# Expert loop of an AdaLN block: numbers kept in registers, parts of the last tile not scattered, the last tile finished in two halves

## The chip, the cores and the metric

One NeuronCore of a Trainium2 chip runs the whole program as one launch. The metric is the device time of a launch in microseconds. The program was run three times for its times, and once more with the hardware profiler on.

## The reference

The block takes 4096 tokens of 256 channels. It applies a modulated layer norm and a linear attention over two key/value sets, adds the gated result to the tokens, applies a second modulated layer norm and then a mixture of experts:

```
scores = sigmoid(xf @ gate_w + bias)
top_scores, top_idx = top_k(scores, 2)          # 8 experts, 2 for each token, weights normalised
up  = xf @ up_w[e] + up_b[e];  hact = gelu(up)   # 256 -> 1024
eo  = hact @ down_w[e] + down_b[e]               # 1024 -> 256
combined = sum over e of 0.1 * w[token, e] * eo[token, e]
shared   = 0.1 * (gelu(xf @ sw_up + sb_up) @ sw_down + sb_down)
out = shared + combined;  out = out / (max(|out|) + 1e-6)      # the maximum over the channels of a token
x   = x + gate * out
```

The maximum makes the last step need a token's whole sum: the shared part and both experts' parts.

## The kernel before, in words

Earlier phases leave in DRAM, for each expert, a region with the rows of its tokens (`expert_in`, 256 channels and 16 numbers of metadata: the token, its eight weights, where its part goes, and at which rows its two copies stand). They leave the shared part of each token in the first half of a row of `shared_part` (`sx`, two times 256 channels) and zeros in the second half; `out` already holds the tokens before the last addition.

The last phase goes over tiles of 256 rows, one expert after the other. An expert's last tile is moved back so that it ends with the expert's rows, and rows that the tile before has already handled are masked. With 8192 rows there are at least FULL = 32 tiles and at most ET = 39; how many there are is known only at run time. Tables made on the chip (`etab` expert, `ktab` its rank, `stab` weight slot or 2 for "not needed", `rtab` row, `ntab` next expert, `vtab`) tell each engine what tile j is. An engine reads one number with `entry`, which is a register load from the table, a register operation on it and a range assertion, all at line 981. `tiles` (L1760) lays out the tiles for each engine: four in line, a loop for tiles 4 to 29, two in line, and then tiles 32 to 38, nested, each inside an `If` on `stab[j]`: `unneeded(j)` (L1785) guards the wind-up `last(j)`, `needed(j)` (L1781) guards `body(j)`. With these inputs tiles 0 to 33 are needed, so the last tile is 33.

The five queues, each in program order, for a tile j with u = j % 2:

- SP loads rows (L985) and metadata (L988).
- TensorE in `body(j)` computes the up products of tile j+1 (`up`, L1870), then four transposes for tile j+2 (`turn_h`, L1842) and the down products of tile j (`down`, L1895), into `psY`.
- ScalarE in `body(j)` first does `part_out(j-1)`: after `yc` it scales by the token's weight into `ys` (L1952). Then come `chunks(j+1)`: gelu (L1933), a rounded copy `gTh` (L1938), and `high` (L1926).
- VectorE in `body(j)` first does `start`: `result(j-1)`, which reads `psY` and adds the bias into `yc` (L2019), and `total(j-1)`, which sums the two halves of the gathered row into `bs` (L2026) and adds the weighted `yc` into `sm` (L2032, once for each 128 rows). Then `end`: low parts `gTl` of the next tile (L1998), between them `largest(j-1)` (`top`, L2037 to L2041) and `gated(j-1)` (`fin`, L2046), then `low(j+2)` (L1993), then `targets(j)`: the row numbers `widx` and `oidx` (L2007 to L2013).
- GpSimd in `body(j)` waits for `ix_ok`, `y_ok` and `g_in`, scatters `ys` of tile j into `shared_part` (L2132, one indirect DMA for each 128 rows), gathers the rows of tile j+1 into `gx` (L2123, likewise two), waits until `fin` of tile j is there and adds it into `out` (L2142, likewise two).

A row goes into `out` only where this tile holds the token's second expert; where it holds the first, its part goes to `shared_part`, so that the tile with the second finds it there. When the first tile of an expert is gathered, `vtab` makes the gather wait for the scatter of the tile before; within an expert it doesn't, since a token is there once. After the last needed tile, VectorE's `last` does `start` and `end`, ScalarE's `last` does `part_out`, and GpSimd's `last` waits until all has landed.

## Time and profile before

| | us |
|---|---|
| median of 3 runs | 898.3 |
| lowest, highest | 893.7, 900.07 |
| the profiled execution | 894.99 |
| its span, first to last instruction | 893.2 |
| mean granted TensorE clock | 0.981 of full |

The span is what the trace covers; all starts in the rows below are microseconds from its beginning. PE is TensorE (PEld its weight loads), DVE VectorE, ACT ScalarE, POOL GpSimd. A `q` behind an engine's name (DVEq) is its sequencer, which runs register, branch and semaphore instructions and is not counted as busy.

### The profile page before, as it was taken

How to read it: one execution, taken by the hardware profiler on the slowest of the kernel's cores; microseconds unless marked ns; L12 is line 12 of the kernel's file. 1: busy time of each engine (PE TensorE's matmuls, PEld its weight loads, DVE VectorE, ACT ScalarE, POOL GpSimd, SP SyncE). 2: the span in 40 equal slices, each digit the busy share in tenths (PEclk: the TensorE clock that was granted, in tenths of full speed). 3: DMA queues.
4: the chain of work that ended last, by engine and by line, in shares of the span. 5: the costliest groups of instructions: out<-in, count | busy, mean ns of one | idle time of the engine just before them, and what ended most of it. 6: DMA issues, size and time to landing. Idle time of an engine off the chain costs nothing.

```text
span 893.2 us, 21239 instructions
## 1 busy us (share of the span) xinstructions
PE 838.0 (94%) x5989; PEld 777.0 (87%) x5990; DVE 632.6 (71%) x1663; ACT 473.9 (53%) x880; POOL 404.9 (45%) x415
## 2 busy tenths in 40 slices
PE   5999999899999999999989999989999999999982
PEld 5778887788888888889789999989999999999982
DVE  5788977568877677687867666666666666666663
ACT  3865654254544544445457665555555556665540
POOL 4553310211451441441701666654666665666665
PEclk9999999899999999999999999999999999999996
DMA  8220000471241231230671333352444433344542
GB/s 294 73 95 1 1 1 0 121 215 25 98 121 26 98 104 39 100 91 32 220 262 53 96 85 97 90 183 55 92 92 95 93 93 89 75 85 91 98 99 51
DMA packets 68607, 83.30 MB, mean 93 GB/s; under 512 B 23088, under 2 KB 56842, under 8 KB 68400
## 3 DMA queue, kind: packets, MB, share of 16 engines
q0 software_dynamic: 25792, 39.92, 19.2%
q1 hardware_dynamic: 41920, 41.64, 15.0%
q8 instruction: 37, 0.61, 0.3%
q10 hardware_dynamic: 816, 0.79, 0.3%
q14 instruction: 42, 0.34, 0.1%
HBM read 45.44 MB, written 41.55 MB: 97 GB/s over the span
## 4 chain that ended last, share of the span: by engine, by line
PE 27%; issue 6%; DVE 5%; DMA 4%; ACT 3%; DVEq 2%; POOL 2%; ACTq 1%; POOLq 0%
PE psUp L1870 14%; PE psY L1895 12%; DMA gx<-shared_part,meta 3%; DVEq L981 1%; ACT gu L1933 1%; DMA shared_part<-ys,widx 1%; PE psH L1842 1%; DVE gTl L1998 1%; POOL out L2142 1%; ACT gTh L1938 1%; DVE top L2037 1%; DVE yc L2019 1%; POOL shared_part L2132 0%; DVE bs L2026 0%; DVE eT L1993 0%
## 5 line engine op out<-in xcount | busy, mean ns | idle before, releaser
L1870 PE MATMUL psUp<-eT,wup 128*128 128x256 f32 x1632 | 203.2, 284 | 6.0 <-DVE eT L1993 5.5
L1870 PEld LDWEIGHTS psUp<-eT,wup 128*128 128x128 f32 x1632 | 198.5, 192 | 7.7 <-issue 6.0
L1895 PE MATMUL psY<-wdn,gTh 128*128 128x256 f32 x1088 | 200.5, 286 | 0.0
L1895 PEld LDWEIGHTS psY<-wdn,gTh 128*128 128x128 f32 x1088 | 169.4, 192 | 0.0
L1895 PE MATMUL psY<-wdn,gTl 128*128 128x256 f32 x544 | 154.3, 284 | 0.0
L2142 POOL DMA_INDIRECT out<-fin,oidx x68 | 109.4, 1609 | 23.5 <-issue 15.5
L1952 ACT ACTIVATE ys<-yc,meta 128x256 f32<-128x256 f32 x68 | 30.9, 502 | 162.6 <-DVE yc L2019 162.6
L1933 ACT ACTIVATE gu<-psUp,ubias 128x256 f32<-128x256 f32 x272 | 113.4, 468 | 6.6 <-DVE gTl L1998 4.1
L1998 DVE TENSOR_TENSOR gTl<-gu,gTh 128x512 fp32r<-128x512 f32 x136 | 93.7, 689 | 26.0 <-ACT gTh L1938 23.6
L2123 POOL DMA_INDIRECT gx<-shared_part,meta x68 | 68.6, 1009 | 84.8 <-DMA shared_part<-ys,widx 63.4
L2132 POOL DMA_INDIRECT shared_part<-ys,widx x68 | 71.4, 1049 | 76.6 <-ACT ys L1952 40.0
L1895 PEld LDWEIGHTS psY<-wdn,gTl 128*128 128x128 f32 x544 | 104.2, 192 | 0.0
L1161 PE MATMUL psU<-h2T,su 128*128 128x512 f32 x384 | 100.3, 399 | 0.0
L1173 PE MATMUL psY<-sd,ghi 128*128 128x256 f32 x512 | 96.8, 288 | 3.0 <-DVE glo L1404 3.0
L1252 ACT ACTIVATE gf<-psU,sbu 128x512 f32<-128x512 f32 x64 | 44.1, 690 | 100.6 <-PE psU L1161 93.3
L1173 PEld LDWEIGHTS psY<-sd,ghi 128*128 128x128 f32 x512 | 81.8, 191 | 8.9 <-DVE glo L1404 5.9
L1674 POOL DMA_INDIRECT expert_in<-h,post x64 | 65.7, 1026 | 52.5 <-DVEq L1476 30.2
L1938 ACT CAST gTh<-gu 128x512 fp32r<-128x512 f32 x136 | 84.4, 621 | 4.3
L1161 PEld LDWEIGHTS psU<-h2T,su 128*128 128x128 f32 x384 | 68.9, 189 | 13.3
L1173 PE MATMUL psY<-sd,glo 128*128 128x256 f32 x256 | 72.8, 284 | 0.0
L2019 DVE TENSOR_TENSOR yc<-psY,dbias 128x512 f32<-128x512 f32 x34 | 23.5, 691 | 67.3 <-issue 63.5
L611 PE MATMUL psG<-xn,kn 128*128 128x257 f32 x256 | 61.5, 389 | 0.8 <-DVE kn L780 0.8
(303 smaller groups left out, 1376.2 us busy)
## 6 DMA issues: line engine op xcount, KB each, us to landing
hin<-expert_in SPq DMA_DIRECT2D x36, 256.0 KB
X<-in_L_attn_x SPq DMA_DIRECT2D x8, 512.0 KB, 7.6
X<-bo_row POOLq DMA_DIRECT2D x8, 512.0 KB
shared_part<-prow SPq DMA_DIRECT2D x8, 512.0 KB, 6.7
shared_part<-sh SPq DMA_DIRECT2D x8, 512.0 KB
out<-X SPq DMA_DIRECT2D x8, 512.0 KB, 4.3
raw_up<-in_L_ffn_up_w SPq DMA_DIRECT2D x3, 1024.0 KB, 6.0
raw_dn<-in_L_ffn_down_w SPq DMA_DIRECT2D x3, 1024.0 KB, 10.4
```

The lines of the kernel that those rows point to most:

```text
L611: mm = nc.tensor.matmul(psG[:, j, 0:C + 1], kn[:, t, j * P:(j + 1) * P], xn[:, f % XR, t], start=(f == 0 and t == 0), stop=(f == NG - 1 an ...
L1161: mm = nc.tensor.matmul(psU[:, m % 2], su[:, b, k, m * P:(m + 1) * P], h2T[:, r, a, k], start=(n == 0), stop=(n == 5))
L1173: mm = nc.tensor.matmul(psY[:, t // 2, (t % 2) * C:(t % 2 + 1) * C], lhs, sd[:, b, m], start=(m == 0 and t % 2 == 0 and n == 0), stop=(m = ...
L1674: nc.gpsimd.indirect_dma_start(out=hs[:, :], out_offset=bass.IndirectOffsetOnAxis(ap=post[:, r, t, k:k + 1], axis=0), in_=h2[:, r, t], in_ ...
L1870: mm = nc.tensor.matmul(psU[:, c, (m % 2) * TR:(m % 2 + 1) * TR], wup[s][:, a, k, m * P:(m + 1) * P], eT[:, u, b, k], start=(n == 0), stop ...
L1895: mm = nc.tensor.matmul(psE[:, u, h * C:(h + 1) * C], (gTh, gTl)[a][:, u, m, h * P:(h + 1) * P], wdn[s][:, b, m], start=(n == 0), stop=(n ...
L1933: nc.scalar.activation(gu[:, c % 2, m], psU[:, c, m * TR:(m + 1) * TR], ACT.Gelu, bias=ubias[:, bass.ds(e * MK + 2 * c + m, 1)]).then_inc( ...
L1938: nc.scalar.copy(gTh[:, u, 2 * c:2 * c + 2], gu[:, c % 2]).then_inc(eu_hi, 1)
L1998: nc.vector.tensor_tensor(gTl[:, u, 2 * c:2 * c + 2], gu[:, c % 2], f32(gTh[:, u, 2 * c:2 * c + 2]), ALU.subtract).then_inc(eu_lo, 1)
L2123: nc.gpsimd.indirect_dma_start(out=gx[:, u, h], out_offset=None, in_=sx[:, :], in_offset=token).then_inc(g_in[u], 16)
L2132: nc.gpsimd.indirect_dma_start(out=sx_half[:, :], out_offset=first, in_=ys[:, u, h], in_offset=None, bounds_check=2 * N - 1, oob_is_err=Fa ...
L2142: nc.gpsimd.indirect_dma_start(out=out[0], out_offset=token, in_=fin[:, u, h], in_offset=None, bounds_check=N - 1, oob_is_err=False, compu ...
```

## The change

A helper `known` reads a table entry for tiles from FULL on once for each engine and keeps the register; later uses take it from there. GpSimd's scatter of parts moves inside the `If` that asks whether the next tile is needed, so the last tile's parts are computed and scattered no more; ScalarE loses its `last`. The semaphore of the gather becomes one for each 128 rows. VectorE's `last` does the last tile in two halves of 128 rows with `finish`, and GpSimd's addition into `out` waits for each half by itself, in every tile. VectorE loads `etab[j]` before `targets(j)` for tiles from 32 on.

```diff
-    g_in = [sem(f"g_in{i}") for i in range(2)]
+    g_in = [[sem(f"g_in{i}{h}") for h in range(2)] for i in range(2)]
...
+    held = {}
+
+    def known(eng, table, j, most):
+
+        if not isinstance(j, int) or j < FULL:
+            return entry(eng, table, j, most)
+        key = (eng.engine, table.name, j)
+        for old in [k for k in held if k[0] == eng.engine and k[2] < j - 2]:
+            del held[old]
+        if key not in held:
+            held[key] = entry(eng, table, j, most)
+        return held[key]
...
     def needed(eng, j):
 
-        return eng.If_ne(eng.to_reg(entry(eng, stab, j, 2)), 2)
+        return eng.If_ne(eng.to_reg(known(eng, stab, j, 2)), 2)
 
     def unneeded(eng, j):
 
-        return eng.If_eq(eng.to_reg(entry(eng, stab, j, 2)), 2)
+        return eng.If_eq(eng.to_reg(known(eng, stab, j, 2)), 2)
...
-                k_exp = entry(pe, ktab, j, E)
+                k_exp = known(pe, ktab, j, E)
                 if isinstance(j, int) and j >= FULL:
-                    return entry(pe, stab, j, 2), k_exp
+                    return known(pe, stab, j, 2), k_exp
...
-            def last(j):
-
-                part_out(j - 1, 1 - j % 2, (j - 1) // 2, entry(act, etab, j - 1, E - 1))
-
             def body(j, u, more, i):
                 new = entry(act, ntab, j, E - 1)
                 if more:
-                    e1 = entry(act, etab, j + 1, E - 1)
+                    e1 = known(act, etab, j + 1, E - 1)
                 if later(j, 1):
-                    part_out(j - 1, 1 - u, i - 1 + u, entry(act, etab, j - 1, E - 1))
+                    part_out(j - 1, 1 - u, i - 1 + u, known(act, etab, j - 1, E - 1))
...
-            tiles(act, body, last)
+            tiles(act, body)
...
             def total(j, u, landed, e):
-                wait(dve, g_in[u], landed)
+                for h in range(2):
+                    wait(dve, g_in[u][h], landed)
...
             def start(j, u, i):
-                e = entry(dve, etab, j - 1, E - 1)
+                e = known(dve, etab, j - 1, E - 1)
                 result(j - 1, 1 - u, e)
-                total(j - 1, 1 - u, 32 * i + 32 * u, e)
+                total(j - 1, 1 - u, 16 * i + 16 * u, e)
+
+            def finish(j, u, landed, h, e):
+
+                done = 3 * j + 3 * h
+                wait(dve, g_in[u][h], landed)
+                if not h:
+                    wait(dve, s_ok, 2 * j)
+                    wait(dve, f_s, 2 * j)
+                nc.vector.tensor_tensor(bs[:, h], gx[:, u, h, C:2 * C], gx[:, u, h, 0:C], ALU.add).then_inc(b_ok, 1)
+                wait(dve, ey_ev, j + 1)
+                wait(dve, b_ok, j + 1 + h)
+                nc.vector.scalar_tensor_tensor(sm[:, h], yc[:, h], meta[:, u, h, bass.ds(e + 1, 1)], bs[:, h],
+                                               ALU.mult, ALU.add).then_inc(s_ok, 1)
+                wait(dve, s_ok, 2 * j + h + 1)
+                nc.vector.tensor_reduce(top[:, 0, h:h + 1], sm[:, h], AX.X, ALU.max, apply_absolute_value=True
+                                        ).then_inc(f_c, 1)
+                wait(dve, f_c, done + 1)
+                nc.vector.tensor_scalar(top[:, 0, h:h + 1], top[:, 0, h:h + 1], EPS, None, ALU.add).then_inc(f_c, 1)
+                wait(dve, f_c, done + 2)
+                nc.vector.reciprocal(top[:, 1, h:h + 1], top[:, 0, h:h + 1]).then_inc(f_c, 1)
+                wait(dve, f_c, done + 3)
+                nc.vector.scalar_tensor_tensor(fin[:, u, h], sm[:, h], top[:, 1, h:h + 1], gate_fb[:],
+                                               ALU.mult, ALU.mult).then_inc(f_s, 1)
 
             def last(j):
 
-                start(j, j % 2, j // 2)
-                end(j, j % 2, False)
+                u, i = j % 2, j // 2
+                e = known(dve, etab, j - 1, E - 1)
+                result(j - 1, 1 - u, e)
+                for h in range(2):
+                    finish(j - 1, 1 - u, 16 * i + 16 * u, h, e)
...
+                if isinstance(j, int) and j >= FULL:
+                    known(dve, etab, j, E - 1)
                 targets(j, u, i)
                 ahead(j, new, (1,))
...
             def body(j, u, more, i):
+                def parts():
+                    wait(pool, y_ok, 2 * j + 2)
+                    for h in range(2):
+                        wait(pool, g_in[u][h], 16 * i + 16)
+                    for h in range(2):
+                        first = bass.IndirectOffsetOnAxis(ap=widx[:, u, h:h + 1], axis=0)
+                        nc.gpsimd.indirect_dma_start(out=sx_half[:, :], out_offset=first, in_=ys[:, u, h], in_offset=None,
+                                                     bounds_check=2 * N - 1, oob_is_err=False).then_inc(w_st[u], 16)
+
                 wait(pool, ix_ok, 2 * j + 2)
-                wait(pool, y_ok, 2 * j + 2)
-                wait(pool, g_in[u], 32 * i + 32)
...
                 if not isinstance(j, int) or j + 1 < FULL:
+                    parts()
                     gather(j + 1, 1 - u, i + u)
                 elif more:
                     with needed(pool, j + 1):
+                        parts()
                         gather(j + 1, 1 - u, i + u)
-                wait(pool, f_s, 2 * j + 2)
                 for h in range(2):
+                    wait(pool, f_s, 2 * j + 1 + h)
                     token = bass.IndirectOffsetOnAxis(ap=oidx[:, u, h:h + 1], axis=0)
...
                 for u in range(2):
-                    wait(pool, w_st[u], 32 * ((j + 1 - u) // 2))
+                    wait(pool, w_st[u], 32 * ((j - u) // 2))
```

## Rows read from the trace of the kernel before

**Rows 1.** Busy time by stretch: engines in us (instructions), granted clock, DMA share, GB/s

```profile
750.00:800.00 50.00, 50.00 (x419) 49.89 (x418) 33.33 (x76) 29.82 (x67) 30.76 (x26) 1.00 0.41 87
...
874.00:893.20 19.20, 2.99 (x26) 2.79 (x24) 5.18 (x14) 0.91 (x2) 10.11 (x8) 0.66 0.33 59
```

**Rows 2.** Waits, 650 to 850 us: total us, times, longest

```profile
POOL gx L2123 <- DMA shared_part<-ys,widx: 33.3, 16, 2.5
```

**Rows 3.** Chain that ended last, VectorE's sequencer ahead of tile 32's yc: start, us

```profile
865.01 0.29 DVEq L981
...
865.62 0.06 DVEq L1785
...
866.16 0.45 DVEq L981
...
867.61 0.31 DVEq L981
...
868.25 0.02 DVEq L82
...
868.43 0.70 DVE yc L2019
```

**Rows 4.** Timeline of TensorE, tiles 32 and 33: start, length, idle before

```profile
853.93 5.99 PE L1870 MATMUL psUp<-eT,wup 128*128 128x256 f32 x48 [0.36 <-issue]
...
869.13 0.63 PE L1842 MATMUL psH<-ident,hin 128*128 128x128 f32 x4 [3.03 <-issue]
...
876.71 0.28 PE L1895 MATMUL psY<-wdn,gTl 128*128 128x256 f32 x1
```

**Rows 5.** Timeline of GpSimd from 865 us

```profile
865.83 1.58 POOL L2142 DMA_INDIRECT out<-fin,oidx  x1 [0.30 <-issue]
871.03 1.04 POOL L2132 DMA_INDIRECT shared_part<-ys,widx  x1 [3.62 <-ACT ys L1952]
...
873.71 1.00 POOL L2123 DMA_INDIRECT gx<-shared_part,meta  x1 [0.30 <-issue]
875.01 0.96 POOL L2123 DMA_INDIRECT gx<-shared_part,meta  x1 [0.30 <-issue]
...
878.21 1.59 POOL L2142 DMA_INDIRECT out<-fin,oidx  x1 [0.30 <-issue]
...
885.90 1.58 POOL L2142 DMA_INDIRECT out<-fin,oidx  x1 [1.41 <-DVE fin L2046]
887.78 1.57 POOL L2142 DMA_INDIRECT out<-fin,oidx  x1 [0.30 <-issue]
```

**Rows 6.** Timeline of VectorE, tile 33's last steps

```profile
881.26 0.69 DVE L2026 TENSOR_TENSOR bs<-gx 128x512 f32<-128x512 f32 x1 [3.42 <-DMA gx<-shared_part,meta]
882.17 0.88 DVE L2032 SCALAR_TENSOR_TENSOR sm<-yc,meta,bs 128x256 f32<-128x256 f32 x2 [0.22 <-DVE bs L2026]
883.09 0.69 DVE L2037 TENSOR_REDUCE top<-sm 128x2 f32<-128x512 f32 x1
883.81 0.17 DVE L2039 TENSOR_SCALAR top<-top 128x2 f32<-128x2 f32 x1
...
884.21 0.88 DVE L2046 SCALAR_TENSOR_TENSOR fin<-sm,top,gate_fb 128x256 f32<-128x256 f32 x2
```

**Rows 7.** Group of VectorE from 560 us, shapes apart: busy us, mean ns

```profile
L2032 DVE SCALAR_TENSOR_TENSOR sm<-yc,meta,bs 128x256 f32<-128x256 f32 x54 | 23.8, 481 | 9.1 <-DVE bs L2026 8.9 <-issue 0.2
```

**Rows 8.** Gather's landing, min/median/max: tile gx from 874 us, then from 560

```profile
DMA to landing us min/median/max: 4.2/5.2/6.2
...
DMA to landing us min/median/max: 3.3/3.5/7.0
```

**Rows 9.** Lines L981 and L1781 from 840 us: ns min/median/max, first and last start

```profile
L981 POOLq TENSOR_LOAD <-stab x9: 284/289/524, 858.1 to 891.9; - x9
...
L1781 POOLq COMPARE_BRANCH  x6: 34/40/55, 859.0 to 892.5; - x6
L1781 PEldq COMPARE_BRANCH  x3: 66/66/5494, 852.2 to 875.7; - x3
```

More of the change, by code:

```diff
@@ L1916, in ahead @@
                     k = entry(act, ktab, j, E)
-                    slot = entry(act, stab, j, 2)
+                    slot = known(act, stab, j, 2)
                     if later(j, 1):
@@ L1985, in ahead @@
                     k = entry(dve, ktab, j, E)
-                    slot = entry(dve, stab, j, 2)
+                    slot = known(dve, stab, j, 2)
                     for s in range(2):
@@ L2123, in gather @@
                     nc.gpsimd.indirect_dma_start(out=gx[:, u, h], out_offset=None, in_=sx[:, :], in_offset=token
-                                                 ).then_inc(g_in[u], 16)
+                                                 ).then_inc(g_in[u][h], 16)
             def body(j, u, more, i):
-                wait(pool, ix_ok, 2 * j + 2)
-                wait(pool, y_ok, 2 * j + 2)
-                wait(pool, g_in[u], 32 * i + 32)
-                for h in range(2):
-                    first = bass.IndirectOffsetOnAxis(ap=widx[:, u, h:h + 1], axis=0)
-                    nc.gpsimd.indirect_dma_start(out=sx_half[:, :], out_offset=first, in_=ys[:, u, h], in_offset=None,
-                                                 bounds_check=2 * N - 1, oob_is_err=False).then_inc(w_st[u], 16)
+                def parts():
[6 more added lines that the diff above has]
+                                                     bounds_check=2 * N - 1, oob_is_err=False).then_inc(w_st[u], 16)
+                wait(pool, ix_ok, 2 * j + 2)
                 if not isinstance(j, int) or j + 1 < FULL:
+                    parts()
                     gather(j + 1, 1 - u, i + u)
```

## The prediction

> **What bounds the kernel now.** I read the busy times by stretch first. In the expert loop TensorE is busy 50.00 of 50 us, and behind 874 us it is busy 2.99 of 19.2 us [rows 1]. So there are two regimes: up to TensorE's last tiles only what shortens or delays its stream counts; behind them only the chain from tile 32's result to the last landing.
>
> The loop's waits come next. GpSimd spends up to 2.5 us in a tile on the landing of a scatter, 33.3 us in 16 tiles [rows 2]. It has slack there, and a few sequencer instructions in it are absorbed.
>
> The chain of waits for the end shows what the tail is made of. Tile 32's `yc` begins at 868.43, though TensorE had stopped at 866.10 (869.13 less 3.03) [rows 3, 4]; the sequencer of VectorE was reading table numbers from 865.01 on. From `yc` the chain goes to ScalarE's `ys`, to the scatter of tile 32 at 871.03, to the gathers of tile 33 at 873.71 and 875.01 [rows 5], to their landing 6.2 us behind the second issue [rows 8], to VectorE's last steps from 881.26 [rows 6], and to two additions into `out`, 885.90 and 887.78. The last is issued at 889.35 and the span ends at 893.2.
>
> **The change, part by part.** All in us of this execution, whose own time is 894.99 for a span of 893.2.
>
> *Registers, TensorE.* Ahead of tile 33's up products it stands 0.36 on issue, in which it reads numbers for `needed(32)` and for the tile [rows 4]. `stab[32]` is held by then, and one read is about 0.6 (865.01 to 865.62 on VectorE, [rows 3]), more than the gap. All behind it comes 0.36 earlier.
>
> *Registers, VectorE.* Between `targets(32)` and `yc` it reads `stab[33]` for `unneeded` (0.61, 865.01 to 865.62), jumps (0.54 to 866.16), reads `stab[33]` again with its branch and `ntab[33]` (together 1.45 to 867.61; at 0.61 for the second, 0.84 for the first) and `etab[32]` (0.64 to the wait ahead of `yc` at 868.25) [rows 3]. The three reads of held numbers go, about 2.0 net of the branches, which stay; `ntab` stays. Ahead of `targets` one read goes (`unneeded` of the body) and one comes (`etab[32]`): zero. So `yc` could start at 868.43 - 0.36 - 2.0 = 866.05. TensorE's results are there at 866.10 - 0.36 = 865.75, so it just doesn't become the limit. GpSimd doesn't either: its addition for tile 31 is issued by 867.41 [rows 5], and the scatter, 2.60 behind `yc`, would start at 868.65. I take 2.4 for this part. If all reads hid behind something it would be 0; it can't be above 2.68, where TensorE limits (868.43 to 865.75).
>
> *The scatter of tile 33 and ScalarE's `last`.* Two issues and a `ys` go. By themselves they give nothing: GpSimd had finished them and stood 1.41 idle until `fin` [rows 5]. They have to go for the next part, since they wait for both gathers.
>
> *Two halves.* The two gathers of tile 33 land 4.2 and 6.2 behind their issues, the least and the most of two [rows 8], at 877.9 and 881.2. The steps of 256 rows take 3.83 from the start of `bs` to the end of `fin`, then 0.81 to the first addition, which is 1.58 long, 0.30, and the second starts 6.52 behind `bs` [rows 5, 6]. For a half: `sm` and `fin` have their width already, 0.48 each [rows 7]. `bs` and the reduction run over 512 columns in 0.69 and the two small steps, at two columns, in 0.17 each [rows 6]; halving what is above 0.17 gives 0.43 for each (bounds 0.35, half, and 0.48, the nearest row of this width). With 0.22 ahead of `sm` and 0.03 between the others: 0.43 + 0.22 + 0.48 + 0.03 + 0.43 + 0.03 + 0.17 + 0.03 + 0.17 + 0.03 + 0.48 = 2.50, bounds 2.34 to 2.60. The first half takes 877.9 to 880.4 and is hidden: the second lands 0.8 later. Its addition is issued while the second half is computed. The second starts 2.50 + 0.81 = 3.31 behind its landing in place of 6.52. That is 3.2 less. For this tile 33's `yc` must be ready with the first landing, at 875.5 on the shifted scale. It ended at 877.83 before; TensorE saves three reads ahead of tile 33's down products (about 1.9 of its 3.03 idle [rows 4]) and the 0.36, so it ends at 875.5 or earlier. There are 0.8 in hand besides. Of TensorE's clock: behind that idle time the mean grant is 0.66 for the stretch [rows 1]; if with 2 us less idle it stays at full speed, `yc` is earlier still, and that changes nothing, as the gather decides.
>
> *The end.* Behind the last landing GpSimd reads `stab[34]` once more, the load at 891.9, the branch at 892.5 [rows 9]. It is held now: 0.6 less.
>
> *Every tile of the loop.* VectorE waits once more, GpSimd twice more, at 0.02 for such a wait (line 82, [rows 3]), with its register work perhaps 0.05, and `out`'s first half may go a little earlier. Covered by GpSimd's wait for landings [rows 2], and TensorE reads tiles ahead. Without that cover it would be 0.1 to 0.2 a tile, 3 to 6 over 30 tiles. I take 0.
>
> The sum is 2.4 + 3.2 + 0.6 = 6.2: 888.8 for this execution. The median of the three runs, 898.3, is 3.3 above it; taken off the median it is **892.1 us**.
>
> **The rivals.**
>
> *The second gather lands in its ordinary time.* 6.2 is long beside a median of 3.5 [rows 8]; the additions of tile 32 are issued right behind it. If in the new order it lands in 3.5, at 876.1, VectorE is still in the first half until 878.0, the second ends at 880.5, its addition starts at 881.3, and the end is 881.3 + 1.57 + 3.85 (889.35 to 893.2) - 0.6 = 886.1, 7.1 earlier: 891.2. At 7.0 it is 5.4 earlier: 892.9. Only the size changes.
>
> *The gathers land together.* Then the halves run one behind the other: the second `fin` 5.0 behind the landing, its addition at 5.8, against 6.5: only 0.7 from this part, 3.7 in all, 894.6. The two landings of this trace are 3.3 apart, against it.
>
> *The reads weren't in the way.* If something else holds `yc` or the scatter of tile 32, only the end's parts stay: 3.8, 894.5. For it speaks that TensorE's results are only 2.3 earlier than `yc`; against it that no other queue shows an instruction due in between.
>
> *Slower: the jumps of VectorE cost a fetch.* `unneeded` jumps over `last`, whose code about doubles, once ahead of tile 32's body and once ahead of tile 33's. Such a jump costs 0.5 now [rows 3]; TensorE's branch over the unused tiles stood 5.5 [rows 9]. At 5.5 instead of 0.5 both would hold `yc`: the one ahead of tile 33 by 5.0 directly; the one ahead of tile 32 by between 0 and 5, since its delay has to come through the low parts of tile 33; I take 3. Against 6.2 that is 1.8 slower, 900.1. It decides once what the jumps add on this path is over 6.2. The 0.5 of today speak against it, with a short distance even when doubled.
>
> The Trainium skill, page "Runtime: NRT & Kernel Launch", section on instruction fetch mechanics, says that a taken branch whose target lies outside the two pages held forces a fetch before the engine goes on. By that rule TensorE's 5.5 was such a fetch and VectorE's 0.5 was not, and a `last` twice as long would still lie inside them; the trace doesn't show the pages themselves.
>
> **How the numbers follow.** The forecast has 0.45, the ordinary or late landing 0.2, landings together 0.08, reads not in the way 0.15, jumps 0.05, a loop that isn't covered, which gives back 3 to 6, 0.07. The cases run from 891.2 to 894.6 on the scale of the median; the three runs lie from 4.6 below to 1.8 above it, and the profiled one 3.3 below. So the range reaches from 887.5 to 897.5. A change of 1%, 9 us, is about what the measurement can tell from none: the forecast's 0.7% is below it. Faster by over 1% needs a low draw of the runs on top, 0.13; slower by over 1% needs the jumps and a high draw, 0.04; within 1%, 0.83.
>
> **What would show it.** TensorE's gap ahead of tile 33's up products gone; no second and third `stab` read on VectorE, `yc` of tile 32 some 2.4 earlier and within 0.4 of TensorE's last matmul; two L2132 issues fewer; `bs` twice at 128 rows' width, the first some 3 ahead of the second; the first addition issued before the second half's `fin`; 3.3 from the last landing of the gather to the last addition. The prediction is wrong if `yc` of tile 32 stays where it is behind TensorE, if both halves start together, or if TensorE is busy for less than 50.00 of 50 us in the loop.

## The result and the profile after

| | before | changed | ratio, 95% interval |
|---|---|---|---|
| median of 19 runs each, us | 897.36 | 891.74 | 0.994 [0.9919, 0.996] |
| lowest, highest | 892.05, 902.58 | 885.95, 895.78 | |
| the profiled execution, and its span | 894.99, 893.2 | 895.78, 893.9 | |

The changed kernel is 5.6 us faster (5.4 by the ratio, 3.6 to 7.3 by its interval). Forecast were 6.2, and 892.1 us.

The profiled execution of the changed kernel is its slowest of 19, so spans mislead. TensorE ends tile 32 at 872.13 in it against 866.11 before, and in a second profile of the same changed kernel at 866.66. The line of the up products shows where that comes from (ns min/median/max, first to last start), before, changed, and the second profile of the changed kernel:

```profile
L1870 PE MATMUL psUp<-eT,wup x1632: 274/283/552, 457.1 to 859.6; 128*128 128x256 f32 x182
...
L1883 PE MATMUL psUp<-eT,wup x1632: 274/283/445, 460.4 to 865.7; 128*128 128x256 f32 x182
...
L1883 PE MATMUL psUp<-eT,wup x1632: 274/283/577, 457.0 to 860.2; 128*128 128x256 f32 x182
```

Of the 6.0, 3.3 are there before the loop's first up product, in phases that the change doesn't touch. The other 2.7 arise inside the loop, and only 0.6 in the second profile. The change does add waits in every tile, but the kernel with held registers alone, whose loop is that of before, is 1.3 longer there too, and all fourteen profiles of this document lie between 402 and 405. So no profile shows a difference of the loop that is larger than its spread. I compare the **tail**: from TensorE's last matmul of tile 32 to the end of the span. It is 27.1 before and 21.8 after (20.1 in the second profile).

The stretches first, a slice of the loop and the tail; they answer to [rows 1], columns as there:

```profile
750.00:800.00 50.00, 50.00 (x419) 49.85 (x418) 33.17 (x79) 28.03 (x62) 31.13 (x27) 1.00 0.42 91
...
872.20:893.90 21.70, 7.88 (x52) 7.71 (x52) 10.03 (x27) 1.50 (x3) 11.84 (x9) 0.71 0.38 58
```

The tail of the kernel before, by the same view:

```profile
866.20:893.20 27.00, 7.86 (x52) 7.68 (x52) 9.42 (x23) 2.40 (x5) 13.68 (x11) 0.69 0.31 52
```

The loop is as full as before, 50.00 of 50. In the tail ScalarE has two instructions less (3 for 5) and GpSimd two (9 for 11), which are the parts of tile 33; VectorE has four more, those of the second half.

The chain that ended last, after (start, us, what), answers to [rows 3]:

```profile
872.13 2.00 issue
874.12 0.70 PE psH L1855 x4
874.83 7.19 PE psY L1908 x48
...
882.16 0.09 DVE yc L2028
882.25 0.52 issue
882.77 0.43 DVE bs L2084
```

This is not the chain of the forecast. It doesn't go through the gather's landing: TensorE stands 2.00 on issue, computes tile 33's down products, and its result starts the first half.

The timeline of TensorE and VectorE, after, answers to [rows 4, 6]:

```profile
860.02 5.92 PE L1883 MATMUL psUp<-eT,wup 128*128 128x256 f32 x48
...
874.12 0.70 PE L1855 MATMUL psH<-ident,hin 128*128 128x128 f32 x4 [2.00 <-issue]
...
872.31 0.69 DVE L2028 TENSOR_TENSOR yc<-psY,dbias 128x512 f32<-128x512 f32 x1 [1.44 <-PE psY L1908]
...
882.16 0.69 DVE L2028 TENSOR_TENSOR yc<-psY,dbias 128x512 f32<-128x512 f32 x1 [3.67 <-PE psY L1908]
882.77 0.42 DVE L2084 TENSOR_TENSOR bs<-gx 128x256 f32<-128x256 f32 x1
...
884.78 0.48 DVE L2097 SCALAR_TENSOR_TENSOR fin<-sm,top,gate_fb 128x256 f32<-128x256 f32 x1
885.18 0.42 DVE L2084 TENSOR_TENSOR bs<-gx 128x256 f32<-128x256 f32 x1
...
887.18 0.48 DVE L2097 SCALAR_TENSOR_TENSOR fin<-sm,top,gate_fb 128x256 f32<-128x256 f32 x1
```

No idle is noted before the up products any more (0.36 before). Tile 32's `yc` starts 0.18 behind TensorE's end, against 2.32 before. The two `bs` are 2.41 apart with no idle between the halves.

GpSimd's timeline, after, answers to [rows 5]:

```profile
874.86 1.04 POOL L2171 DMA_INDIRECT shared_part<-ys,widx  x1 [1.32 <-ACT ys L1965]
876.21 1.02 POOL L2171 DMA_INDIRECT shared_part<-ys,widx  x1 [0.30 <-issue]
877.54 0.99 POOL L2161 DMA_INDIRECT gx<-shared_part,meta  x1 [0.30 <-DVE fin L2056]
878.84 0.96 POOL L2161 DMA_INDIRECT gx<-shared_part,meta  x1 [0.30 <-DVE oidx L2022]
...
886.06 1.69 POOL L2185 DMA_INDIRECT out<-fin,oidx  x1 [2.43 <-DVE fin L2097]
888.45 1.55 POOL L2185 DMA_INDIRECT out<-fin,oidx  x1 [0.70 <-issue]
```

The gather's landing in the end, its least, median and most, answers to [rows 8]:

```profile
DMA to landing us min/median/max: 3.4/3.4/3.4
```

GpSimd's last read of a table number and its last branch, after, answer to [rows 9] (ns min/median/max, first to last start). They are the first two lines; the third is TensorE's second branch past the up products of the unneeded tile 34:

```profile
L981 POOLq TENSOR_LOAD <-stab x1: 283/283/283, 878.5 to 878.5; - x1
...
L1794 POOLq COMPARE_BRANCH  x1: 55/55/55, 893.2 to 893.2; - x1
...
L1874 PEldq COMPARE_BRANCH  x2: 218/1037/1856, 871.6 to 871.9; - x2
```

The read is made at 878.5 and no longer behind the last landing (891.9 before).

From these rows the way to the last addition splits exactly, all counted from TensorE's last matmul of tile 32:

| step | before | changed | second profile of it | forecast difference |
|---|---|---|---|---|
| second gather issued | 8.90 | 6.71 | 6.77 | -2.0 |
| its landing | 6.2 | 3.4 | 4.7 | 0 |
| from there to the last `bs` | 0.05 | 2.94 | 0.49 | 0 |
| last `bs` to last addition | 6.52 | 3.27 | 3.27 | -3.2 |
| last addition starts | 21.67 | 16.32 | 15.23 | -5.3 |

(Forecast -2.0 is the 2.4 without the 0.36 that lies ahead of this origin.) The sum is right within 0.1 in the first profile by luck: two things that were not forecast cancel, a landing 2.8 shorter, and 2.9 in which the landed second half waits for VectorE. In the second profile they don't, and the last addition is 6.4 earlier in place of 5.3.

### The profile page after: what moved, and what is told of

Same layout as the page of the kernel before. It is cut to its first block and busy times, and to the rows that moved or that the text cites. A ratio compares the mean times of both kernels' runs of the same rounds, so it can differ in the third digit from the quotient of the medians.

```text
span 893.9 us, 21242 instructions
## 1 busy us (share of the span) xinstructions
PE 843.5 (94%) x5989; PEld 781.6 (87%) x5990; DVE 631.6 (71%) x1667; ACT 473.1 (53%) x878; POOL 404.0 (45%) x413
## 5 line engine op out<-in xcount | busy, mean ns | idle before, releaser
L1946 ACT ACTIVATE gu<-psUp,ubias 128x256 f32<-128x256 f32 x272 | 113.4, 468 | 10.1 <-DVE gTl L2007 8.6
L2007 DVE TENSOR_TENSOR gTl<-gu,gTh 128x512 fp32r<-128x512 f32 x136 | 93.7, 689 | 18.6 <-ACT gTh L1951 15.6
L1173 PEld LDWEIGHTS psY<-sd,ghi 128*128 128x128 f32 x512 | 80.7, 188 | 10.1 <-DVE glo L1404 7.3
L1659 POOL TENSOR_SCALAR rs<-mv 128x4 f32<-128x4 f32 x16 | 5.5, 344 | 129.0 <-DVE mv L1376 113.6
```

What stands on the lines that cost most here:

```text
L1173: mm = nc.tensor.matmul(psY[:, t // 2, (t % 2) * C:(t % 2 + 1) * C], lhs, sd[:, b, m], start=(m == 0 and t % 2 == 0 and n == 0), stop=(m = ...
L1946: nc.scalar.activation(gu[:, c % 2, m], psU[:, c, m * TR:(m + 1) * TR], ACT.Gelu, bias=ubias[:, bass.ds(e * MK + 2 * c + m, 1)]).then_inc( ...
L2007: nc.vector.tensor_tensor(gTl[:, u, 2 * c:2 * c + 2], gu[:, c % 2], f32(gTh[:, u, 2 * c:2 * c + 2]), ALU.subtract).then_inc(eu_lo, 1)
```

## The experiments

The ratios below are of launches, against the kernel before on the same chip. The kernels ran in three groups, each on a chip of its own: a1 to e3, e4 to e8, e9 to e12; after the result itself the changed kernel ran again only in the first group. The tail and what it holds come from one profile of each kernel, counted as above, in us:

| kernel | ratio, 95% | tail | `yc` of 32 | TensorE's gap | down products of 33 | `yc` of 33 | the gather's landings, least and most | last addition |
|---|---|---|---|---|---|---|---|---|
| before | 1 | 27.1 | 2.32 | 3.0 | 7.9 | 11.0 | 4.2, 6.2 | 21.7 |
| changed | 0.994 [0.9919, 0.996] | 21.8 | 0.18 | 2.0 | 7.9 | 10.0 | 3.4, 3.4 | 16.3 |
| a1_again | 0.9943 [0.9917, 0.9969] | 20.1 | 0.24 | 2.1 | 6.4 | 8.6 | 4.0, 4.7 | 15.2 |
| e1_regs | 0.995 [0.9924, 0.9977] | 22.5 | 0.96 | 1.5 | 6.4 | 8.0 | 3.4, 3.6 | 17.7 |
| e2_halves | 0.9952 [0.9922, 0.9983] | 23.7 | 2.41 | 3.2 | 7.9 | 11.2 | 4.2, 6.1 | 18.3 |
| e3_parts | 0.9986 [0.9956, 1.0016] | 25.3 | 2.13 | 2.8 | 6.4 | 10.3 | 4.6, 5.3 | 19.9 |
| e4_pe_reads | 0.998 [0.9949, 1.0011] | 23.4 | 0.16 | 3.3 | 8.8 | 12.3 | 3.4, 3.4 | 18.6 |
| e5_pe_early | 0.9961 [0.9932, 0.999] | 22.7 | 0.15 | 3.3 | 7.9 | 11.3 | 3.4, 4.2 | 17.6 |
| e7_pe_gather | 0.9989 [0.9961, 1.0018] | 23.0 | 0.16 | 3.2 | 6.4 | 9.8 | 3.5, 4.6 | 16.1 |
| e8_sums_first | 0.9974 [0.9951, 0.9997] | 23.6 | 0.15 | 3.3 | 7.8 | 11.2 | 3.4, 4.2 | 16.7 |
| e9_sums_after | 0.9916 [0.9881, 0.995] | 22.2 | 0.71 | 1.9 | 7.9 | 12.0 | 3.5, 4.2 | 17.4 |
| e10_sums_gather | 0.9936 [0.9903, 0.9968] | 20.6 | 0.60 | 1.5 | 6.4 | 8.0 | 3.7, 4.0 | 13.5 |
| e11_reads_ahead | 0.9956 [0.9925, 0.9988] | 20.7 | 0.15 | 1.9 | 6.4 | 8.5 | 4.8, 5.0 | 15.9 |
| e12_fall_through | 0.9943 [0.9908, 0.9978] | 21.3 | 0.81 | -0.1 | 6.4 | 7.4 | 3.6, 5.8 | 16.4 |

Between two profiles of the very same changed kernel the second landing differs by 1.3 and the down products by 1.5, so a tail alone tells no difference below some 2 us; the steps inside it do. The intervals are 5 to 7 us wide: apart from the sign against before, most of these kernels are not told from each other.

**The changed kernel again.** No edit.

> The changed kernel once more, for a second profile. Tail = from the end of TensorE's last matmul of tile 32 to the end of the span: 27.1 us before, 21.8 in the changed kernel's profile. Theory: the tail is set by tile 33's result, which TensorE finishes 10.7 behind its own last matmul of tile 32, so 21 to 22.5 again, whatever the second gather's landing does between 3.4 and 5. Rival (the landing sets it): the tail follows the landing one for one and is above 23 if the landing is 6.2 as in the profile before. Ratio to the kernel before 0.992 to 0.996.

Its last steps: TensorE's restart, the two `yc` and the two `bs` (timeline):

```profile
868.76 0.63 PE L1855 MATMUL psH<-ident,hin 128*128 128x128 f32 x4 [2.10 <-issue]
...
875.29 0.69 DVE L2028 TENSOR_TENSOR yc<-psY,dbias 128x512 f32<-128x512 f32 x1 [2.25 <-PE psY L1908]
876.20 0.43 DVE L2084 TENSOR_TENSOR bs<-gx 128x256 f32<-128x256 f32 x1 [0.22 <-DMA gx<-shared_part,meta]
...
878.62 0.42 DVE L2084 TENSOR_TENSOR bs<-gx 128x256 f32<-128x256 f32 x1
```

Here the first half does wait for its gather, by 0.22, and the second only for VectorE, 0.49 behind its landing (4.7). So the same kernel falls on either side of the forecast's condition. The tail, 20.1, is below the 21 to 22.5 that were expected: the down products took 6.4 in place of 7.9.

**Held registers alone**, on the kernel before:

```diff
-                    return entry(pe, stab, j, 2), k_exp
+                    return known(pe, stab, j, 2), k_exp
```
and so on all engines, as in the change.

> The kernel before with the held registers alone (and the earlier read of the last tile's expert number). Theory: yc of tile 32 starts 0.2 behind TensorE in place of 2.3, the read at the end goes (0.6), the 0.36 gap goes; tail 22 if the second gather lands in 3.4, 24.4 if in 6.2; about 3 us of the launch, ratio 0.9965. Rival (the reads were not in the way): yc unchanged, tail 27.1, ratio 1.000.

Timeline and the gather's landing, held registers alone:

```profile
872.69 0.63 PE L1855 MATMUL psH<-ident,hin 128*128 128x128 f32 x4 [1.45 <-issue]
...
872.20 0.69 DVE L2032 TENSOR_TENSOR yc<-psY,dbias 128x512 f32<-128x512 f32 x1 [1.49 <-PE psY L1908]
...
882.41 0.69 DVE L2039 TENSOR_TENSOR bs<-gx 128x512 f32<-128x512 f32 x1 [2.50 <-DMA gx<-shared_part,meta]
...
DMA to landing us min/median/max: 3.4/3.5/3.6
```

0.5% faster, interval clear of 1. TensorE's gap ahead of the up products is gone. `yc` of tile 32 starts 1.36 earlier, 0.96 behind TensorE's end and not 0.2 as expected. Of the tail's 4.6, 2.6 is the second landing (3.6 for 6.2); the rest, 2.0, is the 1.36 and the read at the end. With the 0.36 ahead of the tail that makes 2.3 for this part, where 3.0 were forecast (2.4, and 0.6 at the end).

**Halves alone**: the changed kernel, every number read again.

```diff
-        if not isinstance(j, int) or j < FULL:
+        if True:
             return entry(eng, table, j, most)
```
and without VectorE's early read of `etab[j]`.

> The changed kernel with every number read again (no held registers, no extra early read): halves and the dropped scatter alone. Theory: yc of tile 32 again 2.3 behind TensorE, then two half chains of 2.4 each; tail 23 to 24, about 3 us of the launch, ratio 0.9965. Rival (the halves only queue up behind each other): 0.7 us, tail 26.4, ratio 0.999.

This run has the landings of the kernel before, 4.2 and 6.1, and so tests the part under the conditions it was priced for: the last addition starts 3.3 earlier (18.34 for 21.67), against 3.2 forecast. `bs` of the second half waits for its gather, 0.72 behind the first half; 0.8 was forecast (timeline, halves alone):

```profile
881.51 0.42 DVE L2084 TENSOR_TENSOR bs<-gx 128x256 f32<-128x256 f32 x1 [0.72 <-DMA gx<-shared_part,meta]
```

**Parts of the last tile gone, alone**: halves alone, but with VectorE's `last` and the wait for `fin` as before.

```diff
-                for h in range(2):
-                    finish(j - 1, 1 - u, 16 * i + 16 * u, h, e)
+                start(j, j % 2, j // 2)
+                end(j, j % 2, False)
```

> The kernel before with only the last tile's parts not computed and not scattered (gather semaphores split, but VectorE waits for both, last tile whole). Theory: nothing for the two issues and the ys themselves, since GpSimd stood idle behind them: tail 27.1 with a second landing of 6.2, 24.3 with one of 3.4. Rival (their traffic or their issue was on the path): at least 1 us less than that for the same landing.

0.9986, an interval on both sides of 1: nothing measurable. The tail is 1.8 shorter in its profile, as much as the second landing, here 4.6 and the shorter of the two, is below the 6.2 of before (1.6).

**TensorE alone reads again**, the other engines hold.

```diff
-        if not isinstance(j, int) or j < FULL:
+        if not isinstance(j, int) or j < FULL or eng.engine == nc.tensor.engine:
```

> The changed kernel with TensorE alone reading every number again. Its gap ahead of tile 33's down products was 2.0 and 2.1 us in two profiles of the changed kernel, 3.0 to 3.2 where it reads. Theory (tile 33's result from TensorE is on the path now): gap 3.0 to 3.2, tile 33's yc 1.0 later, tail 21.2 to 23 against 20.1 and 21.8, a result that comes after the gather's first landing. Rival (the gather's landing sets the first half, TensorE has slack): gap longer, tail as in the changed kernel.

0.998: most of the gain is gone, though its interval overlaps the changed kernel's. In the profile both landings are 3.4, as in the first profile of the changed kernel, and the last addition is 2.3 later: 1.3 more in the gap, and 0.9 in the down products, whose granted clock was 0.69 in the mean and not 0.78. The 1.3 are the reads; that the 0.9 come of them is not shown, since other kernels with a gap of 2.8 and 3.2 had these products in 6.4. Expected was `yc` of tile 33 1.0 later; it is 2.3 later.

**TensorE's branch earlier.** The reads for tile j+2 stand behind the up products, and one branch goes past those of the unneeded tile:

```diff
-                if more:
+                if more and isinstance(j, int) and j >= FULL:
+                    with needed(pe, j + 1):
+                        up(j + 1, 1 - u)
+                elif more:
                     up(j + 1, 1 - u)
+                if isinstance(j, int) and FULL <= j + 2 < ET:
+                    known(pe, stab, j + 2, 2)
+                    known(pe, ktab, j + 2, E)
                 down(j, u, more, i)
```

> The changed kernel with TensorE's two reads for the next tile but one moved ahead of the down products, and the up products of an unneeded tile skipped with one jump in place of two. Theory: the gap is reads plus jumps less the 2 us that the sequencer is ahead; two reads less take 1.3 off, gap 0.7 or less, and the clock doesn't fall in tile 33's down products; yc of tile 33 starts 7 to 8 behind TensorE's last matmul of tile 32 (10.0 and 8.6 before), and then the gather's landing sets the first half: tail 19 to 20. Rival (the jump is a code fetch that starts only when the branch is reached and takes 1.9 wherever the reads are): gap stays at 1.8 to 2.0, tail 20 to 22.

The branch, as the row of its line (ns min/median/max, first to last start); for the first profile of the changed kernel it stands above. Before:

```profile
L1861 PEldq COMPARE_BRANCH  x2: 218/445/672, 866.3 to 866.6; - x2
```

the second profile of the changed kernel:

```profile
L1874 PEldq COMPARE_BRANCH  x2: 218/1094/1969, 866.2 to 866.5; - x2
```

TensorE alone reading again:

```profile
L1874 PEldq COMPARE_BRANCH  x2: 215/430/646, 872.1 to 872.3; - x2
```

the branch earlier:

```profile
L1794 PEldq COMPARE_BRANCH  x2: 66/1697/3328, 865.6 to 865.7; - x2
```

Its length is not a property of the branch. In these kernels, the earlier it starts the longer it stands: 0.65 if it starts 0.76 behind TensorE's last matmul of tile 32, 0.67 at +0.50, 1.86 at -0.22, 3.33 at -1.78. It ends 1.4, 1.2, 1.6 and 1.6 behind that matmul. In the nine other profiles of kernels that have such a branch it ends 1.1 to 1.8 behind. Within these 0.7 its length varies at one and the same start: 1.97 in the second profile of the changed kernel and 1.31 with registers alone, both started 0.15 ahead of the matmul's end. So the branch was started 1.6 earlier than in the changed kernel and nothing came of it; the two reads, now behind it, are paid in full, and the gap is 3.3 instead of 2.0 (timeline of this kernel):

```profile
870.78 1.08 PE L1855 MATMUL psH<-ident,hin 128*128 128x128 f32 x4 [3.27 <-issue]
```

Expected were 0.7 or less, and 1.8 to 2.0 by the rival; neither came. The two reads cost more than the tail shows: TensorE has two gaps before tile 32's end that the changed kernel lacks, 0.60 ahead of its transposes at 836.75 and 0.30 at 849.18. The next two kernels, which have the same edit, lose 0.8 and 0.7 in this way.

**That, and the gather ahead of the scatter** where the next tile is the same expert's; each of GpSimd's last tiles then holds the gather's code twice. The core of the edit (the waits move with it, and `landed` is read ahead of both):

```diff
+                        with pool.If_eq(pool.to_reg(landed), 32 * (j // 2)):
+                            gather(j + 1, 1 - u, i + u, True)
                         parts()
-                        gather(j + 1, 1 - u, i + u)
+                        with pool.If_ne(pool.to_reg(landed), 32 * (j // 2)):
+                            gather(j + 1, 1 - u, i + u, landed)
```

> As e5, and for tiles from 32 on GpSimd issues the next tile's gather ahead of the scatter of parts where both tiles are of one expert. Theory: the gathers of tile 33 are issued at 1.7 and 3.0 behind TensorE's last matmul of tile 32 in place of 5.4 and 6.7, landed by 5 to 8, and tile 33's first half starts with yc; the last addition starts at 13.7 to 14.5 (16.3 and 15.2 in the changed kernel), tail 18.3 to 19.5. Rival (GpSimd's queue is full: tile 32's additions hold the last one): last addition not before the end of the four issues ahead, tail as e5.

**And the sums ahead of `yc`**: in VectorE's `last` both `bs` come before the result of TensorE is awaited, so that little is left behind it (they go from `finish`).

```diff
+                for h in range(2):
+                    wait(dve, g_in[1 - u][h], 16 * i + 16 * u)
+                    nc.vector.tensor_tensor(bs[:, h], gx[:, 1 - u, h, C:2 * C], gx[:, 1 - u, h, 0:C], ALU.add
+                                            ).then_inc(b_ok, 1)
                 result(j - 1, 1 - u, e)
```

> As e7, and the two sums of the gathered halves (bs) of the last tile are made ahead of yc. Theory: both are hidden by TensorE's last products, each half chain is 0.6 shorter; the last addition starts at 12.9 to 13.5, tail 17.5 to 18.7; ratio to the kernel before 0.989 to 0.992. Rival (a late landing of a gather holds yc, which waits behind the sums in VectorE's queue): tail 19 or more in a profile with a landing over 5.

Both fall short: 0.9989 and 0.9974, where 0.989 to 0.992 was expected of the second. With the gather first the two landings are done well ahead of TensorE's result, so TensorE alone sets when the halves start. But its gap is 3.2 and 3.3 here, as with the branch earlier, and the last addition starts at 16.1 and 16.7, where 13.7 to 14.5 and 12.9 to 13.5 were expected. From there to the end it takes 7.0 and 6.9 where the changed kernel takes 5.5 and 4.9, for the reason shown below with the third kernel that has this gather.

**The sums ahead of `yc` only**, on the changed kernel. The same edit.

> The changed kernel with the last tile's two sums of the gathered rows (bs) made ahead of yc; TensorE and GpSimd as in the changed kernel. Theory: TensorE's result for tile 33 comes 8.6 to 10.0 behind its last matmul of tile 32 and the last addition starts 5.5 behind yc (6.3 and 6.6 in the changed kernel): tail 19.1 to 20.9. Rival (the second gather's landing, 3.4 to 6.2, now holds yc too): with 6.2 yc starts only at 13.5 and the tail is 23 to 24.

The best ratio, 0.9916 in 7 runs, but its interval holds the changed kernel's ratio. Its profile shows the price of the order: the second `bs` waits for the landing and holds `yc` behind it, at 12.0, though TensorE was done at 9.7. The tail, 22.2, is above the 19.1 to 20.9 expected.

**The sums and the gather, TensorE as in the change.**

> As the kernel before it in this list, with the gather of tile 33 ahead of the scatter of tile 32's parts. Theory: the gathers land by 8, ahead of TensorE's result in any case, so the tail is 19.1 to 20.9 whatever the landing takes. Rival (GpSimd's additions for tile 32, ready by then, or something ahead of them are pushed back and hold the last tile's): last addition later than 5.7 behind yc.

Its last addition starts earliest of all, at 13.5, but the tail, 20.6 and inside the 19.1 to 20.9 expected, is not the shortest. GpSimd's last branch, over the code of the unused tiles, by its row:

```profile
L1794 POOLq COMPARE_BRANCH  x1: 50/50/50, 882.5 to 882.5; - x1
```

The span ends at 885.3: 2.8 behind that branch's start, against 0.7 in the changed kernel (893.2 to 893.9). GpSimd's sequencer has no instruction between that branch and 885.1. The code that this branch goes past has become longer by the second copy of the gather in each tile, and the other two kernels with that copy show the same 2.8 (891.4 to 894.2, and 891.5 to 894.3); in all eleven profiles without it it is 0.7. So 2.1 of what was gained was given back there. That it is the length of the code, and not another part of this edit, is the likely reading; no run varies the length alone.

**Reads for tile j+2 ahead of the up products.**

```diff
+                if isinstance(j, int) and FULL <= j + 2 < ET:
+                    known(pe, stab, j + 2, 2)
+                    known(pe, ktab, j + 2, E)
                 if more:
                     up(j + 1, 1 - u)
```

> The changed kernel with TensorE's reads of stab and ktab for the tile after next placed ahead of the up products instead of none (they are then the reads that the up products of that tile would do). In all ten profiles so far the second jump over the up products ended 1.1 to 1.8 behind the last matmul of tile 32, wherever it started (from 1.8 ahead to 0.8 behind). Theory (a code fetch whose arrival is set by when the sequencer entered that stretch, so that reads ahead of the jump are free): jump starts 1.3 earlier and ends no earlier, gap 1.7 to 2.3. Rival (jump costs its 1.9 from where it starts): gap 0.7.

The branch started at -0.23 as before and stood 1.80; tile 34's two reads no longer stand in front of it, but tile 35's two have taken their place. It says nothing on an earlier start. The reads were not free either: TensorE stands 0.65 ahead of the up products at 830.38, where the changed kernel has no gap.

**No branch past the up products.** Where tile j+1 isn't needed, `down(j)` comes first in the code, and the other case, `up` and `down`, behind it.

```diff
+                if more and isinstance(j, int) and j >= FULL:
+                    known(pe, ktab, j, E)
+                    known(pe, ktab, j + 1, E)
+                    with unneeded(pe, j + 1):
+                        down(j, u, more, i)
+                    with needed(pe, j + 1):
+                        up(j + 1, 1 - u)
+                        down(j, u, more, i)
+                    return
```

> The changed kernel with TensorE's code for an only or last tile laid out first: if the next tile is not needed, the down products follow without a jump over the up products; otherwise that copy is jumped over. Theory (the fetch belongs to the jump over about 200 instructions): no gap over 0.5 ahead of tile 33's down products, its clock stays up, yc of tile 33 at 6.5 to 7.5; but TensorE stands 1 to 2.5 ahead of tile 33's up products, where it has stood 0 before, so the launch gains at most 2 us over the changed kernel. Rival (the gap is the reads and waits, not the jump): gap of 1.5 or more stays and none appears ahead of the up products.

Timeline and the gather's landing, no branch past the up products:

```profile
851.86 5.99 PE L1883 MATMUL psUp<-eT,wup 128*128 128x256 f32 x48 [0.35 <-issue]
...
863.89 0.63 PE L1855 MATMUL psH<-ident,hin 128*128 128x128 f32 x4
...
877.19 0.42 DVE L2093 TENSOR_TENSOR bs<-gx 128x256 f32<-128x256 f32 x1 [0.98 <-DMA gx<-shared_part,meta]
...
DMA to landing us min/median/max: 3.6/4.7/5.8
```

TensorE's gap is gone, all 2.0 of it, so the branch past that code was its cause: the two reads of tile 34's numbers still stand ahead of the down products. Only 0.35 came back ahead of tile 33's up products, where 1 to 2.5 were expected. But the launches are not faster than the changed kernel's (0.9943, for 0.994 and 0.9943). In the profile the second `bs` now waits for a landing of 5.8: once TensorE's result is early, the gather decides, as the forecast had it, and the late landing is paid.

## Why the prediction was right, point by point

**Size and place.** 5.6 less at the median against 6.2 forecast, 891.74 against 892.1. That the two times lie as near as 0.4 is luck in part: the three runs from which the forecast started had a median of 898.3, and the nineteen have 897.36; from there 6.2 less would be 891.2. The tail is 5.3 shorter in one profile and 7.0 in the other, with 0.36 ahead of it, so it can hold the whole gain; how much of a launch's difference is made elsewhere, two profiles can't say. The two large parts alone are each worth about what was put down: 0.5% is 4.5 us (interval 2.1 to 6.8) for the registers, forecast 2.4, and 0.6 at the end; 0.48% is 4.3 us (1.5 to 7.0) for the halves with the scatter of tile 33 gone, forecast 3.2. The launches can't tell 4.5 from 2.4, or whether the parts add up; the profiles say more.

**Registers.** `yc` of tile 32 was to start 2.0 earlier against TensorE; it starts 2.14 and 2.08 earlier. The gap ahead of the up products, 0.36, is gone. 2.4 forecast, 2.5 measured in these two profiles. `yc` starts 0.2 behind TensorE, inside the 0.4 that was named; the rival that something else held `yc` falls. But it is not always so near: with registers alone it starts 0.96 behind, and in three later kernels 0.60 to 0.81, where VectorE's last read before it, that of `ntab[33]` which stayed, ends 0.4 to 0.6 behind TensorE. With registers alone the part gave 1.7 in place of 2.4, and what held `yc` there is open.

**The scatter of tile 33.** Nothing by itself, as forecast: 0.9986 [0.9956, 1.0016].

**The two halves.** A half takes 2.49 from the start of its `bs` to the end of its `fin` (882.77 to 885.26), 2.50 forecast, and 3.27 for 3.31 from the last `bs` to the last addition. Where the landings were as in the trace of before (halves alone), the part gave 3.3. What failed is one step: "TensorE saves three reads ahead of tile 33's down products (about 1.9 of its 3.03 idle)", and so "the gather decides". (The sum itself, 877.83 less 0.36 and 1.9, gives 875.57, where the forecast wrote 875.5 or earlier.) The idle shrank by only 1.0, to 2.0. I took the whole gap as instructions to be added up, and there is a branch among them. TensorE's reads ahead of that branch, which starts at 866.6, and behind it, in the kernel before:

```profile
L981 PEldq TENSOR_LOAD <-stab x2: 300/304/308, 864.2 to 865.7; - x2
L981 PEldq TENSOR_LOAD <-ktab x1: 307/307/307, 865.0 to 865.0; - x1
...
L981 PEldq TENSOR_LOAD <-ktab x1: 303/303/303, 867.3 to 867.3; - x1
L981 PEldq TENSOR_LOAD <-stab x1: 513/513/513, 868.0 to 868.0; - x1
```

Of the three reads that go, one stood in front of the branch and two behind it; two more in front stay, tile 34's. In the trace of before the branch stood 0.67 and looked cheap. With one read less in front of it, it started 0.7 earlier against the matmul, stood 1.86, and ended no earlier, 1.6 behind the matmul for 1.2. So the read in front gave nothing, the two behind gave their 1.5, and 0.5 was lost on the branch's end. TensorE's result therefore comes at 10.0 and the landings at 8.8 and 10.1: both halves start from TensorE, one right behind the other, with 2.94 between the second landing and its `bs`. Two signs that the forecast named failed with this step: the two `bs` are 2.4 apart and not some 3, and the last addition starts 6.2 behind the last landing (3.8 in the second profile) and not 3.3. The halves run one behind the other, as in the rival "the gathers land together", though here it is TensorE that brings it about. The rival priced it at 3.7 in all, for a landing of 6.2; here the shorter landing paid for the waiting.

The mechanism has a page: the Trainium skill, page "Runtime: NRT & Kernel Launch", section on instruction fetch mechanics, says that a taken branch to code outside the two pages held forces a fetch, and that the engine goes on only behind it. The trace agrees in kind: the branch past one tile's up products stands up to 3.4 (5.5 over the unused tiles, [rows 9]), and falling through in its place costs nothing. That its end stays within 0.7 while its start moves by 2.5 is from the traces alone. No row shows the fetch itself, and why it ends 1.1 to 1.8 behind TensorE's last matmul of tile 32 stays open.

**The clock.** That the down products might "stay at full speed" with less idle: the granted clock in them was 0.78 in the first profile of the changed kernel and 1.00 in the second (0.78 in the one before), with TensorE idle for 2.0 and 2.1 just ahead. The windows over the down products, first profile of the changed kernel:

```profile
874.20:882.00 7.80, 7.80 (x52) 7.60 (x52) 3.58 (x12) 0.59 (x1) 5.65 (x5) 0.78 0.41 88
```

and the second:

```profile
868.80:875.10 6.30, 6.30 (x52) 6.14 (x52) 3.57 (x12) 0.59 (x1) 4.42 (x5) 1.00 0.33 65
```

The same 52 matmuls take 7.8 or 6.3 with a part of them at 1.2 GHz instead of 2.4, or with none. The idle time ahead doesn't tell which it will be. The first window is of the sums ahead of `yc` only, behind 1.9 idle, the second of the first kernel with the gather ahead, behind 3.2:

```profile
872.00:879.80 7.80, 7.80 (x52) 7.63 (x52) 4.55 (x13) 1.15 (x3) 5.25 (x6) 0.78 0.38 67
...
874.40:880.80 6.40, 6.38 (x52) 6.19 (x52) 2.81 (x10) 0.59 (x1) 5.18 (x5) 1.00 0.45 98
```

So 1 us less of idle time can't be credited with the clock, in the forecast or in these kernels. The clock "changes nothing" only while the gather decides; here it was worth up to 1.5.

**The end.** The read is gone. From GpSimd's last wait, for the landing of the last addition, to the end of the span it is 0.9 now (893.0 to 893.9) and was 1.5 (891.7 to 893.2): 0.6 less, as forecast. In the first profile the last landing itself took 0.6 longer and hid it.

**The loop.** TensorE is busy 50.00 of 50, and 150.00 of 150 from 700 to 850: there the added waits are covered. For the loop's first tiles see the 2.7 and 0.6 above.

**The slower rival.** Behind VectorE's jump over `last` ahead of tile 33 its sequencer stood 0.49 before its next instruction (865.67 on), and it stands 0.49 now, with `last` about twice as long; a chance of 0.05 was fair. But such a cost exists in this kernel: GpSimd's last branch took 2.1 more once each tile held a second gather.

**What stays open.** What fixes the end of TensorE's branch; why the second landing takes from 3.4 to 6.2 in kernels with the same order of DMAs; why the sums ahead of `yc` had the best launches with a tail that isn't the shortest; and how far the spread of 10 us between launches is made in the phases ahead.

## What to carry to other kernels

A branch that jumps far isn't priced by its own duration: here an instruction taken away in front of it only lengthened it, and only those behind it came off. Look at when it ends as its start moves, before its neighbours are added up. Where it sits on the path, lay the likely case out to fall through. And when a part makes one of two converging chains shorter, both have to be written down to the same moment with their spread: here 1.5 from the clock and 2.8 from the landing were larger than the 0.8 that I had counted as in hand.

## What the runs showed of the hardware

- A branch of TensorE past one tile's up products stood from 0.49 to 3.42 us and ended 1.1 to 1.8 behind the matmul then running out, in 13 profiles in which it began between 1.8 ahead of that matmul's end and 0.8 behind it.
- A branch of GpSimd over the unused tiles went from 0.7 to 2.8 (to the end of the span) with the edit that gave each tile's code two more indirect DMAs.
- The same 52 matmuls took 6.3 us at a granted clock of 1.00 and 7.8 at 0.78; the longer time came behind 1.9 idle and the shorter behind 3.2, in two kernels.
- The landing of the same gather of 128 rows took 3.4 to 6.2 from its issue, 3.4 and 4.7 in two profiles of one kernel.
- In two executions of one kernel TensorE ended tile 32 at 866.66 and at 872.13, as far apart as the whole change is worth.
